# Splitting the router's second product around two groups of query matmuls

## Time and profile before

| | us |
|---|---|
| median of 3 executions | 1282.16 |
| lowest and highest | 1276.53, 1286.46 |
| span of the profiled execution, 36001 instructions | 1340.9 |

### The profile page before, as it was taken

How to read it: one execution, slowest core, us unless ns; L and a number is a source line. 1 busy time by engine, 2 the same in 40 slices (tenths; PEclk the granted TensorE clock), 3 DMA queues, 4 the chain that set the end, 5 groups by cost and what they waited for, 6 DMA issues and landing times. The chain is left out here.

```text
span 1340.9 us, 36001 instructions
## 1 busy us (share of the span) xinstructions
PE 1224.7 (91%) x11024; PEld 735.1 (55%) x11025; DVE 881.3 (66%) x1933; ACT 722.1 (54%) x1040; POOL 744.6 (56%) x980
## 2 busy tenths in 40 slices
PE   8887999998999989999999986869899999999997
PEld 4445665655655655665655654534354555555454
DVE  4657787877868867867877867545445555555454
ACT  4336875775775775775766662624333333334333
POOL 4003555675675675675675674864644445444545
PEclk9879999999989998989989997889999999999999
DMA  8842664584583574583583573967999989998886
GB/s 267 253 135 65 173 176 153 148 254 142 150 258 130 142 241 152 147 262 131 144 237 115 132 215 109 357 221 156 199 177 184 175 173 188 179 172 155 168 165 133
DMA packets 135547, 239.22 MB, mean 178 GB/s; under 512 B 18440, under 2 KB 49416, under 8 KB 134280
## 3 DMA queue, kind: packets, MB, share of 16 engines
q1 hardware_dynamic: 102391, 161.24, 41.2%
q0 software_dynamic: 29808, 67.73, 25.2%
q10 hardware_dynamic: 3232, 8.68, 1.9%
HBM read 112.00 MB, written 101.40 MB: 159 GB/s over the span
## 5 line engine op out<-in xcount | busy, mean ns | idle before, releaser
L1854 PE MATMUL S<-we_s,wq_s 128*128 x1620 | 376.3, 382 | 12.6 <-DVE att L1832 5.8
L1782 POOL DMA_INDIRECT out<-xn,to x135 | 208.9, 1547 | 212.7 <-DMA out<-xn,to 123.6
L1854 PEld LDWEIGHTS S<-we_s,wq_s 128*128 128x128 f16 x1620 | 158.1, 98 | 180.8 <-issue 22.3
L1172 POOL TENSOR_TENSOR we_s<-P_s,we_s 128x1024 f16<-128x1024 f32 x96 | 204.2, 2136 | 65.6 <-ACT we_s L927 65.3
L1793 ACT ACTIVATE wq_s<-PVp 128x512 f16<-128x512 f32 x137 | 81.6, 597 | 272.4 <-PE PVp L1844 247.1
L1252 POOL DMA_INDIRECT dispatched<-xn,idx x128 | 131.7, 1029 | 92.6 <-ACT xn L620 52.1
L975 DVE TENSOR_REDUCE mx_sb<-S 128x6 f32<-128x924 f32 x160 | 171.3, 1111 | 11.3 <-PE S L726 9.1
L708 PE MATMUL W<-we_s,wq_s 128*128 128x512 f16 x512 | 168.7, 409 | 8.7 <-ACT mT L933 5.3
L746 PE MATMUL W<-wo_s,aT_hi 128*128 128x512 f16 x512 | 164.5, 383 | 2.6 <-DVE aT_lo L953 1.4
L1832 DVE SCALAR_TENSOR_TENSOR att<-S,be_s 128x512 f32<-128x512 f32 x135 | 93.3, 691 | 111.0 <-PE S L1854 101.5
L1810 DVE TENSOR_TENSOR wq_s<-PVp,wq_s 128x512 f16<-128x512 f32 x137 | 94.6, 691 | 38.3 <-ACT wq_s L1793 35.1
(11 more groups left out here) (207 smaller groups left out, 2039.8 us busy)
## 6 DMA issues: line engine op xcount, KB each, us to landing
P_s<-dispatched SPq DMA_DIRECT2D x139, 260.5 KB
we_s<-we_s SPq DMA_DIRECT2D x186, 128.0 KB, 6.0
be_s<-in_x SPq DMA_DIRECT2D x16, 1024.0 KB, 9.1
xR_s<-in_x SPq DMA_DIRECT2D x16, 1024.0 KB
out<-xR_s SPq DMA_DIRECT2D x16, 1024.0 KB
wst<-in_weT SPq DMA_DIRECT2D x16, 512.0 KB, 6.2
we_scratch<-wsp SPq DMA_DIRECT2D x16, 512.0 KB, 5.5
Kst<-k_scratch SPq DMA_DIRECT2D x16, 480.0 KB, 5.1
```

Source lines behind the costliest of these rows:

```text
L1172: e.tensor_tensor(Pst[1][:, r:r + 2, :], exps(n), Pst[0][:, r:r + 2, :], ALU.subtract).then_inc(pldp, 1)
L1782: e.indirect_dma_start(out, bass.IndirectOffsetOnAxis(ap=to[u][:, :], axis=0), yw[u % YW], None, bounds_check=N - 1, oob_is_err=False, com ...
L1854: m = e.matmul(Yp[:, u % 2, :], gT[u % 2][xp][:, k, :], we_s[:, bass.ds(n * WN + (wp * KC + k) * D, D)], start=(c == 0), stop=(c == 11))
```

## The change

`pe_LB` takes a first and a last j. Its waits stand ahead of j = 0 alone, and its signal behind j = 3. In `pe_slot` its first two parts stay where they were (18 matmuls), j = 2 moves behind `Q6` and j = 3 behind `Q7` (9 matmuls each). The call for the last block, outside the slots, asks for all four parts at once. No instruction is added or removed, and no wait.

```diff
-    def pe_LB(e, b, s):
+    def pe_LB(e, b, s, first, last):
         bank = BANK["LB"]
-        e.wait_ge(ate, b.at(4, 4))
-        if b.first:
-            e.wait_ge(p_rx, 5)
-        if free := emptied("LB", s):
-            e.wait_ge(*free)
-        for j in range(NJ):
+        if first == 0:
+            e.wait_ge(ate, b.at(4, 4))
+            if b.first:
+                e.wait_ge(p_rx, 5)
+            if free := emptied("LB", s):
+                e.wait_ge(*free)
+        for j in range(first, last):
...
-        m.then_inc(lbp, 1)
+        if last == NJ:
+            m.then_inc(lbp, 1)
...
         if on_bm1 and not bm1.last:
-            pe_LB(e, bm1, s)
+            pe_LB(e, bm1, s, 0, 2)
         if on_bp2:
             pe_Q(e, bp2, 6, s)
+        if on_bm1 and not bm1.last:
+            pe_LB(e, bm1, s, 2, 3)
+        if on_bp2:
             pe_Q(e, bp2, 7, s)
+        if on_bm1 and not bm1.last:
+            pe_LB(e, bm1, s, 3, 4)
...
-            pe_LB(e, LAST, LAST + (-(-1)))
+            pe_LB(e, LAST, LAST + (-(-1)), 0, NJ)
```

## The result

| | before | after |
|---|---|---|
| median of 20 executions each, us | 1281.22 | 1284.77 |
| lowest and highest | 1275.47, 1289.48 | 1281.01, 1290.78 |
| ratio, with its 95% interval | | 1.0034 (1.0018 to 1.0050) |

The sign and the size are about right. The forecast took about 1% as the least that can be told from no change; over 20 executions each the interval is 0.16% to either side, so this 0.34% is clear of noise. The reason is not the one that the forecast gave, and most of this document is about that.

A forecast was written before the change was run, and what follows sets the result against it. PE, busy 91% of the span, was taken as the bound. Terms 0 + 0 + 6.5 + 0 gave +6.5 us on 1282.2, so 1288.7, say 1288.5; range 1267 to 1305.

The forecast's parts named there:

- No gain in front of Q6: Half of LB ahead of Q6: Q6 waits for ACT's copy mT anyway and can't start sooner; gain 0.
- the hold: PE's signals around PV5, MT and LB come late in twelve slots; laid to the scatter, not LB's length; change 0.
- Rival A: Splitting LB ends the stall that crowded small matmuls cause in twelve slots; -36.0 us, 1246, or 1254; 8%.
- rival B: PE's sequencer runs dry in LB and large matmuls let it refill; -12.1 us, 1270; 10%.
- The size of a slot's piece: 18 LB matmuls moved behind Q6 and Q7, uncovered: 0.45 us a slot, taken as 0.5, at most 0.9.
- The sum, 13 x 0.5 = 6.5 us: Delay of Q8 passes through ACT and DVE back to PE in 13 slots; +6.5 us, 11.7 at the other end.
- rival C: The 0.5 us a slot is swallowed by PE's waits for DVE in front of AT2; 1282; 17%.
- Cost of the late signal of LB: 0: LB ends later, but DVE's wait of 3.16 us for POOL's lgq covers its delayed reduction; cost 0.
- Rival D, the clock: PE idles between LB's first half and Q6, so the clock falls over Q6 to Q8; +23.0 us, 1305; 20%.
- The profile of before as a base: Rows came from a profiled execution some 59 us longer than unprofiled ones; the forecast was called the same either way.

The follow-up runs named there:

- before again: The unchanged kernel, profiled a second time with no edit; ratio 1.0017, span 1278.2 us.
- LB behind, flat: The unchanged kernel with all 36 LB matmuls moved behind Q7 and PE's hardware loop written out; 1278.69 us, ratio 0.9963.
- after again: The changed kernel, timed and profiled a second time with no further edit; 1283.35 us, ratio 1.0024.
- the pair with MT first: MT moved ahead of PV5, in the unchanged kernel (LB whole) and in the changed one (LB split); 1285.06 and 1289.55 us.
- before, flat: The unchanged kernel with PE's hardware loop written out slot by slot; 1278.16 us, ratio 0.9978.
- before, flat and shifted: The unchanged kernel with PE's loop written out and forty unused semaphore increments ahead of PE's code; 1333.36 us, ratio 1.0016.
- The three held kernels: Forty increments ahead of PE's code in the changed kernel unrolled, the unchanged one unrolled, and the changed one with its loop; 1338.64, 1333.36, 1339.50 us.

## Why the prediction was right, and where it was not

**No gain in front of Q6** (forecast: 0). Right on both levels. Q6 comes 1.37 to 1.45 us after MT's start without the hold and 3.66 to 3.81 with it, LB whole or split, as long as MT stands behind PV5. Rival A, which needed the hold to hang on LB, and rival B, which needed the sequencer to run dry in LB, are both dead: the hold comes within the first 18 small matmuls as it did with 36, and without it 36 in a row take 25 ns each. The 62 ns that the forecast weighed, from the Trainium skill's "TensorE: Matmul & The Clock Gate", are in its section "Wait — 56ns, not 53.3ns?" for hardware decode switched off; no run here shows them.

**The size of a slot's piece** (18 x 0.025 = 0.45, taken as 0.5). The stretch MT to ST0 grew by 0.45 us. Right.

**The sum, 13 x 0.5 = 6.5 us.** This is the step that failed, on the level of the result. It let every piece pass through Q8, ACT and DVE back to PE, and looked for what could swallow it at AT2 only (rival C). The waits that swallow it are two others: ST0's own for mT's row, ahead of AT2, and PV0's for POOL, behind it. Both are in the profile of before again with 6.4 and 6.0 us, and most slots keep their 45.8 us with 0.45 or 0.90 us more of uncovered work. LB behind, flat, puts this term at nothing in the whole of the time; the traces leave 0.45 us of it, in slot 1. C was right in kind and wrong in place, so 1282 would be the level without what follows.

**What the 4.4 us are instead.** Two terms that the forecast did not have: the three slots in which a fetch of PE's code makes the last part of mT's rows later, 4.5 us in the profile of after and 3.1 in that of after again, and the turn of PE's loop, 0.6 and 1.1 us. These are differences to one profile of before. That they come near the 6.5 us of the forecast is luck. Not settled are some 2 us of the pair with MT first and what lies outside slots 2 to 12. Slot 12 of after again is 2.1 us longer (47.46 us against 45.36) with no late landing: its granted clock is 0.96, with a stretch at 1.2 GHz that begins 16.4 us after MT, during a wait of 1.28 us for POOL in front of PV0. Slot 9 of before again and slot 10 of before, flat, are like it (47.12 and 46.95 us, 0.96). So such a slot comes in kernels with LB whole too, and one of them more or less is over 1 us in a single profile.

**Cost of the late signal of LB: 0.** Right, and without need of the cover in most slots: DVE comes to the reduction at the same time with LB whole or split, and LB is done by then. Only in slot 12 of after does DVE wait for LB, 1.18 us, and 1.89 us for POOL's lgq behind it.

**Rival D, the clock.** It did not come on the first level: over slots 2 to 12 the granted clock is 0.99 in both. It falls to 0.96 or 0.97 in single slots, behind some of the late landings, behind the turn and around PV0's wait, and so is part of their price. On the second level the profiles can't tell: of the twelve scatter slots ten are below 1.00 in the first profile of before and five in before, flat and shifted, both with LB whole, against ten and nine with the split.

**The hold and the scatter.** The forecast took the hold to belong to the scatter. The scatter is a condition (no slot without one is held) and not the cause: on the first level it stands at the same distance from MT, and nothing is held. What makes the difference between 1283 and 1333 us stays open. The three held kernels ran on another chip (number 15) than the unheld ones of the experiments (5, 8 and 11), so a difference between chips is as possible as one in time.

**The profile of before as a base.** Its span was 59 us above the timed median, and the forecast said so and went on, arguing that the answer is the same with and without a hold. For Q6 this held. But in a held slot mT itself is late and PE is behind, and neither ST0's wait for mT's row nor PV0's for POOL is there, so no view of such a slot could show what takes up the pieces. Nor could slot 1, the one without a hold: it has no scatter, the row lands at 3.56 us, ahead of PE's own 3.97, and there the 0.45 us are paid. The forecast read all its rows from slots in which the term is, or may be, real.

## What to carry to other kernels

Where a profile's span and the timed median differ by some per cent, look for stretches of the trace that are free of the difference, and ask in what else they differ before arguing from them: slot 1 was free of the hold, and of the scatter too. A cost that is added to the busiest engine counts only if no wait behind it on that engine is longer than it; list the waits between the edit and the end of the period before summing. And when moving small work changes the time without changing undisturbed periods, look for the few long ones: here the order of instructions decided when 16 KB of code were fetched, and that decided when a 16 KB transfer was complete.

## What was not expected of the hardware

- A 16 KB packet of PE's instruction queue takes 0.9 to 1.9 us on one DMA engine. In the eight profiles with MT behind PV5 and no hold, it starts 2.2 to 3.3 us after MT in 17 of the slots 2 to 13. There the last of 16 parts of a small transfer lands at 4.56 to 6.53 us, with the other fifteen on time. In 78 of the other 79 slots it lands at 4.05 to 4.88 us, in one at 5.33.
- The turn of PE's hardware loop costs 2.2 to 7.0 us in front of its first matmul, by the order of the work ahead of it (2.31, 2.54, 3.28, 5.60 and 7.00 us in five orders, and 2.2 and 2.8 in two profiles with the hold), and nothing once PE's slots are written out. The two kernels written out whose intervals lie lowest are at 0.9963 and 0.9972 of before.
- PE's signals can be held back for 2.4 us in every slot with a scatter. Before, run beside three other kernels, was at a median of 1333.3 us, and at 1281 to 1285 us in every other group of executions, for one and the same kernel.
